# Keys and values of an attention computed ahead in units and kept in DRAM, with the chain of Q on ScalarE

## The chip, the core and the metric

One core of a Trainium2 chip runs the whole program. TensorE (PE) multiplies, the vector engine (DVE), ScalarE (ACT) and GpSimd (POOL) work on tiles in SBUF (DVE and ACT in PSUM too), and SyncE (SP) issues most DMAs. Each engine takes its instructions in order and waits on semaphores. The metric is the device time of one execution in microseconds (us), lower being better; the time before is the median of three runs.

## The reference, cut to what matters

Four batches of 512 rows of 512, each with a context of 512 rows of 256:

```python
x = x + ssm(ctx, layernorm(x))              # conv, 16 states scanned over 512 steps, 512 channels
x = x + ternary_ffn(layernorm(x))           # 512 -> 2048 -> 512, gelu, rows rounded to 8 bits
x = x + attention(layernorm(x), ctx)
x = x + moe(layernorm(x))                   # 8 experts, top 2, and a shared one

def attention(h, ctx):                      # 16 heads of 128; Wk, Wv: 256 x 2048, Wq: 512 x 2048
    q = rmsnorm((h @ Wq).reshape(B, 512, 16, 128), gq)
    k = rmsnorm((ctx @ Wk).reshape(B, 512, 16, 128), gk)
    v = (ctx @ Wv).reshape(B, 512, 16, 128)
    return softmax(q @ k.T * 128 ** -0.5) @ v @ Wo       # per head, heads joined before Wo
```

Keys and values depend on the context and the weights alone, not on `h`.

## The kernel before, in words

All is float32 but the ternary feed-forward and the experts. The order on each engine is written out by hand; engines meet by semaphores that count the uses of PSUM banks: a ring of two for each of `px`, `ps` (`py`) and `pp`, a `full` and a `drained` count for each bank.

The program has a prologue, four turns (one for each batch) and the mixture of experts. The prologue runs the scan of batch 0 in TC = 8 rounds on DVE (`times_b`, `scans`, `times_c`, for i = 0 and 1), and in each round makes a piece of the ternary weights: `w_sums` on ACT, `ternary` on DVE, `w_turned` on PE, `w_out` on ACT. PE sums the states in `y_sum`. ACT makes the next round's exponentials in `decay`.

A turn b first ends the scan of its batch (`scan_end`), then runs the feed-forward (`in_quant`, `ffn1`, `ffn2_turned`, `ffn2`), with the front of the next batch's scan (`scan_a`, `scan_conv`, `scan_b`, `scan_c`, softplus) between them. Then the attention in NG = 8 groups of GH = 2 heads. `xn_turned` and `xn_out` put the normalised rows, transposed, into `xnT`. In a group, PE makes the rows of Q (`rows`, 32 matmul records of 256 columns), K and V (16 each) in `pp`, transposes K and Q, makes `scores`, `values`, and the `denominators`; and it projects the output of the group before (`out_proj(g, k0, h)`, two tiles in `px`), which DVE adds to `xc` (`add_out`). Around that, DVE copies the rows of Q and K out (`rows_out`), scales Q by the inverse root of its mean square (`mean_square`, `q_scale`), copies Q transposed, adds up the exponentials (`key_sums`) and inverts the denominators (`recip`). ACT squares Q and K, copies V and K transposed, and makes the exponentials, in which the factor of K stands as the scale. POOL raises the mean squares to -0.5 (`row_rms`).

In the three turns that have a next batch, DVE also runs its scan in the same groups: `times_b` and four scans for each of two states, `times_c`, `add_y`. The last turn has none of that. The first group of a turn has its own order and also a norm (`gate_norm` or `moe_norm`).

The weights of the next group are loaded by SP when the rows that used the old ones are `full`; `next_bc` loads the rows of B and C for the next states once `times_c` has read the old ones. All turns but the last are one hardware loop on each engine, and so are groups 1 to 7.

Of the kernel before, what the change touches and what calls it, by code (L numbers as in the profile page):

```python
# [12 lines left out]
F32 = mybir.dt.float32  # L13
# [17 lines left out]
GH = 2  # L31
# [18 lines left out]
SEG_SIZE = {"A": 2, "XQ": 4, "F1": 4, "B": 2, "F2T": 4, "F2": 1, "C": 4, "AP": 4, "W": NT * H, "POST": 4, "TERN": 5 * TC}  # L50
# [24 lines left out]
PP_OFF = {"Q": 0, "K": 2, "V": 4, "KT": 6, "QT": 7, "D": 6 + 2 * GH}  # L75
PP_FIRST = {**PP_OFF, "K": 0, "V": 2, "Q": 3}
PP_STEP = {"KT": 2, "QT": 2}
PP_USES = 6 + 3 * GH
assert PP_USES % 2 == 0


def program(nc, t):
    ctx = ExitStack()
    with ctx:
# [8 lines left out]
        x3_dram = nc.dram_tensor("x3_dram", (B, L, DM), F32).ap()  # L93

# [7 lines left out]
        minus_magic = sb("minus_magic", [P, 1])  # L102
        conv_w = sb("conv_w", [P, EC, DC])
# [50 lines left out]
        qraw, kraw = qk_raw[:, 0], qk_raw[:, 1]  # L154
# [7 lines left out]
        ctx_ssm = dsum  # L162

# [111 lines left out]
        sq_done = sem("sq_done")  # L275
        ssv_done = sem("ssv_done")
# [73 lines left out]
        dram = t  # L350

# [27 lines left out]
        def _(sp):  # L379
# [16 lines left out]
            def bc_store(s, turn_):  # L396
                if not isinstance(s, int):
# [12 lines left out]
            def w_load(which, g):  # L410
                name, dst, s, chunk = {"k": ("Wk", wk, wk_in, CC), "q": ("Wq", wq, wq_in, NC), "v": ("Wv", wv, wv_in, CC)}[which]
                src = dram[name].rearrange("(c p) w -> p c w", p=P)
                sp.dma_start(dst[:], src[:, :, bass.ds(g * GW, GW)]).then_inc(s, 16)

# [22 lines left out]
            def pair(j, which):  # L437

                for odd in range(2):
                    r = j * 2 + odd  # L440
                    sp.wait_ge(stage_used[odd], j)
                    w_stage(r, odd, which)
                    for i in range(GH):
                        sp.wait_ge(hc_done[i], r)
                        bc_load(bc_first[odd][:, i], (bc_odd_in if odd else bc_in)[i], r * GH + i)
# [1312 lines left out]
```

## Time and profile before

| | us |
|---|---|
| median of 3 runs (2214.78 to 2217.63) | 2215.62 |
| the profiled execution, its own time | 2218.66 |
| its span, first to last instruction | 2216.7 |
| PE busy | 1985.3 (90%) |
| DVE busy | 1661.4 (75%) |
| ACT busy | 953.3 (43%) |
| POOL busy | 172.7 (8%) |
| DMA moved | 122.79 MB |
| mean granted TensorE clock | 0.939 |

The span is what lies inside the trace; the execution's own time has 2.0 us more around it. Busy shares are means over stages with different limits, so the rows further down are cut by stage. In the trace a float32 matmul of 512 columns is two records of 0.43 us start to start; their durations overlap. A helper issues most matmuls, so that their line is always L1334, and the tiles tell them apart.

### The profile page before, as it was taken

To read this page: it belongs to the slowest core of one execution; us is meant where nothing else is said; L and a number is where in the kernel's file an instruction comes from. 1 tells how busy PE (TensorE), PEld (TensorE's weight loads), DVE (VectorE), ACT (ScalarE), POOL (GpSimd) and SP (SyncE) were. 2 spreads that over 40 slices of the span, in tenths; PEclk is the share of its full clock that TensorE was granted. 3 is DMA by queue.
4 is the path that set the end of the run, shared out by engine and by line. 5 is a ranking of instruction groups with operands and counts; after the bars stand their busy time and mean duration, and the time that the engine had idled before them with its cause. 6 is when DMAs were issued, how large, how long until landed. Compare 5 with 4: busy or idle time off the path is not lost.

```text
span 2216.7 us, 25518 instructions
## 1 busy us (share of the span) xinstructions
PE 1985.3 (90%) x7548; PEld 1155.7 (52%) x7548; DVE 1661.4 (75%) x2271; ACT 953.3 (43%) x2208; POOL 172.7 (8%) x120
## 2 busy tenths in 40 slices
PE   6545798999989889999898999996899999899999
PEld 2222345656654556656445565662556666454554
DVE  2999567999995789999867999998553434356555
ACT  3544255455543555555346455552443434221221
POOL 0000001100010110100101010010011101000000
PEclk8777898999999999999998999998999999899999
DMA  3223011212111011222101121221122323100100
GB/s 121 76 76 114 10 40 33 72 57 80 62 57 58 32 54 51 77 62 76 67 20 38 54 79 57 76 66 38 48 58 53 75 51 67 48 32 6 39 19 19
DMA packets 90732, 122.79 MB, mean 55 GB/s; under 512 B 8880, under 2 KB 52528, under 8 KB 90176
## 3 DMA queue, kind: packets, MB, share of 16 engines
q1 hardware_dynamic: 79104, 113.89, 16.1%
q0 software_dynamic: 10768, 6.82, 2.2%
q10 hardware_dynamic: 816, 1.57, 0.2%
q8 instruction: 19, 0.31, 0.1%
q14 instruction: 25, 0.20, 0.0%
HBM read 119.90 MB, written 8.65 MB: 58 GB/s over the span
## 4 chain that ended last, share of the span: by engine, by line
issue 37%; PE 34%; DVE 24%; POOL 2%; DVEq 1%; DMA 1%; ACT 1%; POOLq 0%; SPq 0%; ACTq 0%
PE pp L1334 11%; PE px L1334 11%; DVE arena L959 10%; DVE arena L970 5%; PE ps L1334 5%; DVE arena L951 3%; PE pp L1555 2%; PE po L1334 2%; PE pd L1334 2%; DVE dsum L1192 1%; DVE qk_raw L1116 1%; DVE dsum L1188 1%; POOL bc L535 1%; POOL arena L541 1%; POOL rms L554 1%
## 5 line engine op out<-in xcount | busy, mean ns | idle before, releaser
L959 DVE TENSOR_TENSOR_SCAN arena<-arena 128x512 f32<-128x512 f32 x256 | 290.0, 1201 | 1.8
L1334 PE MATMUL px<-wo,oT 128*128 128x512 f32 x512 | 251.7, 616 | 23.6 <-DVE xc L1156 23.2
L1334 PE MATMUL ps<-qkT 128*128 128x512 f32 x512 | 252.9, 605 | 3.3 <-ACT hbuf L798 3.0
L798 ACT ACTIVATE hbuf<-ps,shift,rms 128x512 f32<-128x512 f32 x256 | 198.6, 777 | 127.4 <-PE ps L1334 119.9
L1334 PE MATMUL pp<-wq,xnT 128*128 128x256 f32 x1024 | 237.1, 391 | 2.9 <-issue 1.5
L786 ACT ACTIVATE dsum<-qk_raw 128x128 f32<-128x128 f32 x512 | 151.2, 296 | 185.4 <-DVE qk_raw L1116 185.4
L1156 DVE SCALAR_TENSOR_TENSOR xc<-px,rden,xc 128x512 f32<-128x512 f32 x256 | 187.6, 748 | 41.6 <-PE px L1334 33.7
L1334 PEld LDWEIGHTS pp<-wq,xnT 128*128 128x128 f32 x1024 | 198.0, 196 | 31.2 <-ACT xnT L773 4.1
L554 POOL TENSOR_TENSOR rms<-ssv,minus_half 128x8 f32<-128x8 f32 x64 | 105.0, 1640 | 960.1 <-DVE ssv L1170 960.1
L655 ACT ACTIVATE arena<-arena,a_neg 128x512 f32<-128x512 f32 x256 | 161.3, 709 | 21.5 <-DVE arena L959 16.6
L1334 PEld LDWEIGHTS ps<-qkT 128*128 128x128 f32 x512 | 90.9, 193 | 127.0 <-issue 76.8
L1334 PEld LDWEIGHTS px<-wo,oT 128*128 128x128 f32 x512 | 96.8, 197 | 105.5 <-issue 61.8
L1116 DVE COPY qk_raw<-pp 128x512 f32<-128x512 f32 x128 | 87.8, 686 | 69.9 <-PE pp L1334 69.7
L1334 PE MATMUL pp<-wk,ctx_att 128*128 128x256 f32 x512 | 121.0, 383 | 16.1 <-DVE qk_raw L1116 16.1
L1334 PE MATMUL po<-hbuf,v_sb 128*128 128x512 f32 x256 | 130.7, 592 | 0.0
L869 ACT ACTIVATE oT<-px 128x512 f32<-128x512 f32 x72 | 43.0, 597 | 201.5 <-PE px L1334 201.5
L951 DVE TENSOR_TENSOR arena<-arena,bc 128x2048 f32<-128x2048 f32 x56 | 127.7, 2280 | 2.3 <-DVE v_sb L921 2.0
L1334 PE MATMUL pd<-hbuf,v_sb 128*128 128x512 f32 x256 | 126.0, 615 | 0.0
L1334 PEld LDWEIGHTS pp<-wk,ctx_att 128*128 128x128 f32 x512 | 95.3, 190 | 49.4 <-issue 28.3
L1334 PE MATMUL pp<-wv,ctx_att 128*128 128x256 f32 x512 | 116.8, 380 | 2.6 <-DVE qk_raw L1116 2.5
L970 DVE TENSOR_TENSOR arena<-arena,bc 128x2048 f32<-128x2048 f32 x52 | 118.0, 2274 | 0.0
L977 DVE TENSOR_TENSOR arena<-arena 128x2048 f32<-128x2048 f32 x48 | 110.0, 2291 | 3.4
(198 smaller groups left out, 2972.4 us busy)
## 6 DMA issues: line engine op xcount, KB each, us to landing
bc<-bc_dram SPq DMA_DIRECT2D x56, 512.0 KB, 5.3
wq<-in_Wq SPq DMA_DIRECT2D x32, 512.0 KB, 4.7
wo<-in_Wo SPq DMA_DIRECT2D x32, 512.0 KB, 3.3
hbuf<-in_w SPq DMA_DIRECT2D x8, 1024.0 KB, 5.2
wk<-in_Wk SPq DMA_DIRECT2D x32, 256.0 KB, 2.5
wv<-in_Wv SPq DMA_DIRECT2D x32, 256.0 KB, 2.5
xs<-in_x SPq DMA_DIRECT2D x4, 1024.0 KB, 5.1
xnT<-bc_dram SPq DMA_DIRECT2D x8, 512.0 KB, 7.3
```

Of the source, the lines that this page charges most:

```text
L554: nc.gpsimd.tensor_tensor(rms[:, j], ssv[:, j], minus_half[:, 0:NT * GH], ALU.pow).then_inc(rms_done, 1)
L655: nc.scalar.activation(dA[i][:, e], delta[:, e], ACT.Exp, scale=a_neg[:, e, bass.ds(g * GH + i, 1)]).then_inc(exp_done[i], 1)
L786: nc.scalar.activation(squared[:, i], raw[:, k, h * D:(h + 1) * D], ACT.Square, accum_out=ss[:, j, i:i + 1]).then_inc(sq_done, 1)
L798: nc.scalar.activation(pT[:, h, k], ps[s_use % 2][:], ACT.Exp, bias=shift[:, 0:1], scale=rms[:, 1, k * GH + h:k * GH + h + 1]).then_inc(p_ ...
L951: V.tensor_tensor(hb[i], du, bc_i[:, 0:1, :].broadcast_to((P, EC, L)), ALU.mult).then_inc(dbu_done[i], 1)
L959: V.tensor_tensor_scan(hb[i][:, e], dA[i][:, e], hb[i][:, e], 0.0, ALU.mult, ALU.add).then_inc(scan_done[i], 1)
L970: V.tensor_tensor(dst, hb[i], bc_i[:, 1:2, :].broadcast_to((P, EC, L)), ALU.mult).then_inc(hc_done[i], 1)
L977: V.tensor_tensor(u, u, hb[i], ALU.add).then_inc(y_added, 1)
L1116: V.tensor_copy(dst[:, 2 * j:2 * j + 2, :].rearrange("p t w -> p (t w)"), pp[bank][:]).then_inc(pp_drained[bank], 1)
L1156: V.scalar_tensor_tensor(xc[:, k], px[bank][:], rden[:, h, k:k + 1], xc[:, k], ALU.mult, ALU.add).then_inc(px_drained[bank], 1)
L1334: return nc.tensor.matmul(out, lhsT, rhs, start=first, stop=last, **kw)
L1555: m = nc.tensor.transpose(pp[bank][:, k * P:(k + 1) * P], raw[:, k, h * D:(h + 1) * D], ident[:])
```

## The change

The keys and values of one batch and group are a unit U = 8b + g. A unit makes the rows of K, squares them, makes the rows of V, transposes K, and stores K (transposed, with its gain) and V in DRAM. Twelve units are made in the prologue (one and two per round in turn), four in the feed-forward of each of the first three turns, eight in that of the last. A group loads its two tiles. On ACT, a unit's rows of K are copied out and squared in their PSUM bank; DVE has no part in it. The inverse roots of a turn's units are one POOL instruction.

In a group the rows of Q stay in PSUM; ACT squares them there, makes the mean, scales them from PSUM to SBUF and copies Q transposed. The denominators go to `px`. DVE's order is new. The stages for the stores are `wo` and `wq` in the prologue and `xnT` in a turn. The turns are written out on SP and POOL, the prologue's rounds on all but DVE. PE's order in a turn and in a group, ACT's part of a unit, and SP's:

```diff
+            def kv(U, groups, loads):
+                pe.wait_ge(ctx_att_in, loads * 16)
+                pe.wait_ge(wk_in, U * 16 + 16)
+                for j in range(2):
+                    kv_rows(U, groups, "K", j, wk)
+                pe.wait_ge(wv_in, U * 16 + 16)
+                for j in range(2):
+                    kv_rows(U, groups, "V", j, wv)
+                pe.wait_ge(k_rows, U * 2 + 2)
+                for h in range(GH):
...
+                        m = nc.tensor.transpose(pp[bank][:, k * P:(k + 1) * P], kraw[:, k, h * D:(h + 1) * D], ident[:])
+            for r in range(TC):
+                for U in round_units(r):
+                    kv(U, 0, U // NG + 1)
+                for i in range(GH):
+                    y_sum(r, i)
+                w_turned(r // 2, r % 2, 1 if r < HG else 2)
...
                 if scan:
                     scan_a(b + 1, turn_, 0)
+                    scan_a(b + 1, turn_, 1)
                 scan_end(b, turn_)
                 if scan:
-                    scan_a(b + 1, turn_, 1)
                     scan_conv(b + 1, turn_, 0)
+                kvs(0, 1 if scan else 2)
                 in_quant()
                 ffn1(0)
...
                 ffn1(1)
                 if scan:
                     scan_b(b + 1, turn_)
+                else:
+                    kvs(2, 3)
...
                 ffn2_with_turned(1)
+                kvs(*((1, 2) if scan else (3, 5)))
                 ffn2_with_turned(2)
+                kvs(*((2, 3) if scan else (5, 7)))
                 ffn2(3, 0, 4)
+                kvs(*((3, 4) if scan else (7, 8)))
...
+                    if is_first(g):
+                        xn_turned()
+                        q_rows(0)
+                        q_rows(1)
+                    else:
+                        q_rows(0)
                         out_proj(g - 1, 0, 0)
+                        q_rows(1)
                         out_proj(g - 1, 0, 1)
                         out_proj(g - 1, 2, 0)
                         out_proj(g - 1, 2, 1)
+                    q_turned(0)
+                    q_turned(1)
                     scores(0, 0)
```

```diff
+            def kv_out(U, groups, stages):                  # ACT
+                for j in range(2):
...
+                    nc.scalar.activation(kraw[...], pp[bank][:], ACT.Copy).then_inc(k_rows, 1)
...
+                            m = nc.scalar.activation(slot, slot, ACT.Square, accum_out=ss_k[...])
...
+                nc.scalar.activation(ssv_k[...], ss_k[:], ACT.Identity, bias=eps[:, 0:1], scale=1.0 / D).then_inc(k_means, 1)
+                for j in range(2):
...
+                    nc.scalar.activation(stages[1][...], pp[bank][:], ACT.Copy).then_inc(pp_drained[bank], 1)
+                for h in range(GH):
...
+                    nc.scalar.activation(stages[0][:, h], pp[bank][:], ACT.Copy, scale=kgain[:, 0:1]).then_inc(pp_drained[bank], 1)
...
                 def xn_out():
+                    act.wait_ge(k_stored, units_after(b) * 16)
+                    act.wait_ge(v_stored, units_after(b) * 16)
...
+                        decays(0)                           # a later group
+                        squares(0)
+                        decays(1)
+                        squares(1)
+                        mean_squares()
+                    q_out()
+                    for h in range(GH):
+                        qT_out(h)
                     exps(0)
...
+                    if not (isinstance(g, int) and g == NG - 1):          # SP, in group(g)
+                        sp.wait_ge(ps_full[1], (G + 1) * (GH * NT // 2))
+                        kv_load(G + 1)
+                        sp.wait_ge(po_full, (G + 1) * GH)
+                        v_load(G + 1)
```

DVE in a later group is now `times_b(0)`, `add_out(0, 0)`, `times_b(1)`, `add_out(0, 1)`, `add_out(2, 0)`, `add_out(2, 1)`, `scans(0)`, `key_sums(0)`, `scans(1)`, `key_sums(1)`, `times_c(0)`, `recip(0)`, `recip(1)`, `add_y(0)`, `times_c(1)`, `add_y(1)`. In the first group `gate_norm` stands behind `recip(1)`. In the prologue ACT's round is `w_sums`, `kv_out`, `decay(0)`, a second `kv_out` in every other round, `decay(1)`, `w_out`.

## Rows read from the trace of the kernel before

**Rows 1.** Stretches: prologue, a feed-forward with scan, a group with scan, one without.

```profile
core 0: us, PE busy (x) PEld busy (x) DVE busy (x) ACT busy (x) POOL busy (x), PEclk, DMA share, GB/s
65.00:231.00 166.00, 90.72 (x367) 45.56 (x368) 161.32 (x147) 71.44 (x132) 0.79 (x1) 0.74 0.25 89
231.00:341.00 110.00, 94.71 (x383) 47.86 (x382) 68.75 (x105) 49.30 (x62) 9.31 (x4) 0.90 0.08 28
434.39:473.43 39.04, 38.47 (x146) 24.48 (x145) 37.65 (x46) 20.35 (x57) 3.28 (x3) 1.00 0.23 67
1677.52:1715.75 38.23, 38.22 (x145) 24.56 (x145) 16.38 (x32) 15.45 (x49) 5.50 (x5) 1.00 0.28 62
```

**Rows 2.** Instructions in order of time, PE, end of turn 0's feed-forward (start, duration).

```profile
325.63 3.62 PE L1334 MATMUL pp<-wk,ctx_att 128*128 128x256 f32 x16
...
340.75 9.34 PE L1334 MATMUL pp<-wq,xnT 128*128 128x256 f32 x32 [0.73 <-issue]
```

**Rows 3.** The same view, PE, a steady group with scan.

```profile
482.78 1.04 PE L1555 MATMUL pp<-ident,qk_raw 128*128 128x128 f32 x8
483.66 3.88 PE L1334 MATMUL ps<-qkT 128*128 128x512 f32 x8
...
499.38 7.15 PE L1334 MATMUL pp<-wq,xnT 128*128 128x256 f32 x32
```

**Rows 4.** The same view, ACT, a square and a copy out.

```profile
341.14 0.29 ACT L786 ACTIVATE dsum<-qk_raw 128x128 f32<-128x128 f32 x1
...
483.42 0.69 ACT L792 ACTIVATE qkT<-pp,kgain 128x512 f32<-128x512 f32 x1 [1.91 <-PE pp L1555]
```

**Rows 5.** The same view, PE, start and end of the prologue's rounds.

```profile
69.67 1.02 PE L1334 MATMUL pd<-arena,ident 128*128 128x512 f32 x2
...
233.74 1.88 PE L1334 MATMUL ps<-arena,ident 128*128 128x512 f32 x4
...
237.17 0.27 PE L1412 MATMUL px<-ident,w_scale 128*128 128x128 f32 x1
...
239.53 0.22 PE L1334 MATMUL px<-minus_bf,v_sb 128*128 128x128 bf16 x1
```

**Rows 6.** The same view, ACT, the end of round 1 and what follows.

```profile
107.66 0.60 ACT L682 ACTIVATE ws<-px 128x512 f32 x1 [10.08 <-PE px L1412]
...
110.97 0.63 ACT L670 ACTIVATE qk_raw<-hbuf 128x512 f32<-128x512 f32 x1
```

**Rows 7.** DMA issues: queue, times issued, KB each, median us to landing.

```profile
bc<-bc_dram SPq DMA_DIRECT2D x56, 512.0 KB, 5.3
...
x_dram<-xc SPq DMA_DIRECT2D x4, 1024.0 KB, 7.6
```

**Rows 8.** Instructions in order of time, DVE, group 1 and a steady group.

```profile
393.21 1.40 DVE L1156 SCALAR_TENSOR_TENSOR xc<-px,rden,xc 128x512 f32<-128x512 f32 x2
...
478.16 1.65 DVE L1178 TENSOR_SCALAR qk_raw<-qk_raw,rms 128x128 f32<-128x128 f32 x8
...
482.13 1.61 DVE L1156 SCALAR_TENSOR_TENSOR xc<-px,rden,xc 128x512 f32<-128x512 f32 x2 [0.17 <-PE px L1334]
...
504.69 2.29 DVE L977 TENSOR_TENSOR arena<-arena 128x2048 f32<-128x2048 f32 x1
506.90 0.68 DVE L1116 COPY qk_raw<-pp 128x512 f32<-128x512 f32 x1
```

**Rows 9.** The same view, PE, the last turn's feed-forward.

```profile
1535.87 3.92 PE L1447 MATMUL ps<-ident,hbuf 128*128 128x128 f32 x16 [10.80 <-DVE hbuf L1079]
...
1552.34 1.97 PE L1464 MATMUL ps<-ident,qkT 128*128 128x128 f32 x8 [5.00 <-DVE qkT L1099]
...
1586.63 3.62 PE L1334 MATMUL pp<-wk,ctx_att 128*128 128x256 f32 x16
...
1595.48 7.15 PE L1334 MATMUL pp<-wq,xnT 128*128 128x256 f32 x32 [0.73 <-ACT xnT L773]
```

**Rows 10.** Stretches around a wait of PE (columns as in the first group).

```profile
371.00:375.00 4.00, 1.22 (x9) 0.75 (x7) 3.83 (x7) 0.00 (x0) 0.00 (x0) 1.00 0.00 0
375.00:380.00 5.00, 5.00 (x16) 3.31 (x16) 4.27 (x13) 0.97 (x4) 0.46 (x1) 0.59 0.00 0
```

More of the change, by code:

```diff
@@ L563, in turn @@
                     log_error(b + 1)
-                else:
+                key_rms(units_before(b), units_after(b))
+                if not scan:
                     for i in range(2, 4):
@@ L708, in _ @@
             d_times_u(0)
-            def pair(j, which, last=False):
-                for odd in range(2):
-                    w_sums(j, odd, which)
-                    if not (last and odd):
-                        for i in range(GH):
-                            decay(0, j * 2 + odd + 1, i)
-                    w_out(j, odd, which)
-            with act.Fori(0, HG // 2) as j:
-                pair(j, 1)
-            for j in range(HG // 2, TC // 2):
-                pair(j, 2, last=j == TC // 2 - 1)
+            for r in range(TC):
+                j, odd, which = r // 2, r % 2, 1 if r < HG else 2
+                units = round_units(r)
+                w_sums(j, odd, which)
+                kv_out(units[0], 0, stages_first)
+                if r + 1 < TC:
+                    decay(0, r + 1, 0)
+                for U in units[1:]:
+                    kv_out(U, 0, stages_first)
+                if r + 1 < TC:
+                    decay(0, r + 1, 1)
+                w_out(j, odd, which)
             gate_silu(0, 0)
@@ L843, in group @@
                     exps(1)
+                    if is_first(g) and scan:
+                        d_times_u(b + 1)
                     for h in range(GH):
@@ L1214, in group @@
                             times_b(b + 1, g, 1)
+                        key_sums(G, 0)
+                        if scan:
                             scans(b + 1, g, 1)
-                        key_sums(G, 0)
-                        key_sums(G, 1)
-                        recip(0)
+                    else:
+                        if scan:
+                            times_b(b + 1, g, 0)
+                        add_out(g - 1, 0, 0)
+                        if scan:
+                            times_b(b + 1, g, 1)
+                        add_out(g - 1, 0, 1)
+                        add_out(g - 1, 2, 0)
+                        add_out(g - 1, 2, 1)
+                        if scan:
+                            scans(b + 1, g, 0)
+                        key_sums(G, 0)
+                        if scan:
+                            scans(b + 1, g, 1)
+                    key_sums(G, 1)
+                    if scan:
+                        times_c(b + 1, g, 0)
+                    recip(0)
+                    recip(1)
+                    if is_first(g):
                         if scan:
```

454 lines of the change are left out of this document (244 added, 210 removed).

## Prediction

> **What bounds the kernel now.** I read the stages first. In the prologue the vector engine (DVE) is busy 161 of 166 us and TensorE (PE) 91; in the scan batches' feed-forward stage PE is busy 95 of 110; in a steady attention group with a scan beside it PE is busy 38.5 and DVE 37.7 of 39.04; in the last batch, without a scan, PE is busy all 38.23 [rows 1]. So PE sets the pace of attention, nearly everywhere of the feed-forward, and not of the prologue. Then the instructions in order of time, for what follows what. The chain of waits gives PE 34%, DVE 24% and "issue" 37% of the span, too coarse here.
>
> **The change conserves PE work.** All 32 units of keys and values are still computed: 7.8 us of PE each: K rows 3.62 with their tail of 0.16, so 3.46 [rows 2], V the same, four transposes twice, 0.44 each [rows 3]. It leaves 32 groups and goes to 12 places in the prologue, 3 x 4 in the scan batches' feed-forward, 8 in the last one's. The sum is what each group gives back minus what each place costs.
>
> **A unit's price.** With ScalarE (ACT) free, from the unit's start: K0 to 1.7, K1 to 3.5; ACT takes K0 after 0.17, copies (0.6 to 0.7) and squares four times (0.29 each) [rows 4], so V0 starts only at 4.0, ends 5.7; K1's bank is free at 6.0, V1 ends 7.7; KT0 8.2; KT1 waits for V1's copy and takes 8.6 to 9.1. PE is held 9.1 us for 7.8 of work, ACT 9.9. Squares that read and write PSUM have no row; 0.29 is the SBUF one, bounds 0.2 to 0.4, that is 8.3 to 10 per unit.
>
> **Prologue, 12 units.** PE waits there for `times_c` each round. A round costs it two `y_sum` (3.43 each) [rows 5] and `w_turned`: 2.4 in the last four rounds [rows 5]; in the first four ACT drains it from 107.66 to 110.97 [rows 6], with the transposes ahead 3.7. The first unit stands behind ACT's `w_sums` (four of 0.62) [rows 6] and holds PE 10.2; a second one, behind a `decay`, ends at 20.5. So rounds of one unit take 10.2 + 6.9 + 3.7 = 20.8, of two 31.1; later 19.1 and 29.4 (`w_sums` is shorter). PE becomes the bound: DVE needs about 21 a round. Round 0 starts at 70.7, where the first sums end [rows 5], and takes 9.1 + 6.9 + 3.7 = 19.7; then 31.1 + 20.8 + 31.1 + 19.1 + 29.4 + 19.1 + 29.4 = 180.0, end at 270.4 against 239.7 [rows 5]: **+30.7**. Bounds: with units perfectly packed 12 x 7.8 + 8 x 9.95 = 173, end 243.5, +4; with ACT's two chains serial and some half clock, +45. Filling PE's idle also takes away the half clock after each, which is counted by using full-clock rows. SP's next weights are asked for one phase ahead; the inverse roots of 12 units are one POOL instruction of 96 columns. Now two of 8 columns take 3.28 [rows 1], which makes 1.64 flat to 19.7 by columns, starting some 12 before the end, so even with the diagonals behind it done before the convolution 20 later. Hidden.
>
> **Feed-forward with scan, 4 units.** Unit 0 stands before `in_quant`, where PE has just come from the convolution without a wait; units 1 and 2 between matmuls that followed each other. Nothing covers them: 3 x 9.1 = 27.3 (moving `scan_a` ahead of `scan_end` shifts work only). Unit 3 replaces K rows, V rows and a wait for the norm, from 325.63 to the Q rows at 340.75, 15.1 [rows 2]. New, from the same point: ACT is still in exp and ln, 3.8 more; K0 is taken there, so KT1 leaves PE at 10.9 and ACT at 11.9; `xn_out` now waits until the stores have landed, since `xnT` is their stage: no 512 KB store has a row, 1 MB takes 7.6 [rows 7], so 3.8 to 7.6, I take 4.7; then 2.6 for the copies: 19.2. +4.1. Queued behind that wait on ACT are the squares of Q and the `decay` that DVE's scans want; both are counted below from the Q rows on. `xs` is loaded behind SP's same wait and is wanted 30 later. Sum **+31.4** a batch.
>
> **A group with scan.** DVE loses 4 row copies, 8 scalings, 2 copies of Q, the mean squares: 2.7 + 1.6 + 1.4 + 0.3 = 6.0 (0.68 a copy, 1.65 the scalings) [rows 8]. PE loses 7.8. But PE's filler is gone. From the start of the Q rows, t = 0: `recip(1)` of the group before ends near 0.5; DVE does `add_y`, `times_c`, `add_y`, `times_b`, 2.2 each [rows 8], to 9.45 with their self-waits; `add_out(0,0)` to 10.8; `times_b` to 13.0; its next result frees px0 at 13.8. PE: Q rows and the first `out_proj` to 8.6; then it needs px0, free at 10.2: `out_proj(0,1)` to 12.0; idle to 13.8; then tile by tile with DVE (0.86, hand-over 0.17, 0.75) [rows 8]: `out_proj(2,1)` ends 17.4; transpose and ACT's copy of Q to 18.8; scores, values and denominators 15.7 as before, 483.66 to 499.38 [rows 3]. The loop closes at 34.5, with DVE waiting a microsecond for the last denominator. 39.03 - 34.5 = 4.5 saved. ACT's chain is inside it: squares of Q1 at 8.8 to 10.2, mean 10.4, POOL 1.64 and hand-overs to 12.2, eight scalings 14.4 (0.2 to 0.3 each; no row from PSUM), before 17.4. If it were later by over 3 it would be paid. Seven groups: **-31.5** a batch.
>
> Each unit also stores and loads 1 MB, 64 MB more over the kernel beside 123; in a group the DMA engines are busy 0.23 [rows 1], so the bandwidth is there and only order counts. SP's new waits: V's load waits for the last value product, and `next_bc(0)` is queued behind it, so that row of B and C is asked for at -0.5 instead of -3. It lands after 5.3 alone [rows 7], up to about 7.5 behind V; wanted at 7.2. bc 1, asked for at 5.0, is wanted at 10.8. Taken as just in time.
>
> **First group.** From the start of its Q rows (half clock, as now): scores at 16.9; 15.7 of PE work, plus 1.0 for the `decay` that stands between the two heads' exps, to 33.6; `recip` 0.5, the norm 4.4, three passes and `times_b` at 2.2, `add_out` 1.3: 48.6. Now that `add_out` ends at 394.6, 53.8 after 340.75 [rows 2, 8]. In a steady group it ends at 10.8 in place of 12.3, so 1.5 of the 5.2 is counted there already: **-3.7**, bounds 0 (a chain as long as now) and -7.8 (all PE work given back).
>
> **Last batch.** Units 0 and 1 go into the 10.8 wait [rows 9]: 18.3 plus a cold start, +8.5. Unit 2 into the 5.0 wait [rows 9], but behind a gelu: +4.9. Units 3 to 6: 4 x 9.15 = 36.6. Unit 7 in place of 1586.63 to 1595.48 [rows 9]: 9.9 + 4.4 + 2.3 = 16.6 against 8.9, +7.8. Sum +57.8. Group there: PE Q rows and `out_proj` to 14.1, both transposes and copy of Q to 15.5 (q chain 14.4), then 15.7: 31.2 against 38.23, x 7 = -49.2; first group -1.0. **+7.6**.
>
> **Sum.** 30.7 + 3 x (31.4 - 3.7 - 31.5) + 7.6 = 30.7 - 11.4 + 7.6 = +26.9. The profiled execution took 2218.66 (span 2216.7 and 2.0 around it), so 2245.6; it lay 3.0 over the median of the runs, 2215.62, so **2242**.
>
> **TensorE's clock.** In 371 to 375 PE was busy 1.22; in the 5 us behind it the granted clock was 0.59, 1.2 GHz for most of it [rows 10], against 1.00, 2.4 GHz, through groups with at most 0.57 idle [rows 1]. The new group has idles of 1.7 and 1.8 within five, in between. I take no fall: both are shorter than the one in the rows. The Trainium skill (TensorE: Matmul & The Clock Gate, "A second HAM failure mode: psum-queue depth-cycling") tells of a kernel whose short idles between groups of matmuls, from cycling through PSUM banks, made the clock swing between both levels; that speaks for the third rival.
>
> The Trainium skill (DMA: Bandwidth & Descriptors, "Anatomy of one DMA") gives a fixed 2.0 us plus bytes by 436 GB/s and says most of the fixed part is the write's receipt, longest for HBM; by it a 512 KB store would take 3.2 in place of my 4.7 and each of the four batches would be 1.5 shorter, 6 in all. The 7.6 measured for 1 MB [rows 7] is above the 4.4 that it gives there, so for stores the trace doesn't agree.
>
> **Rivals.**
> 1. The forecast, 2229 to 2257 with its unit bounds: 0.47.
> 2. Faster: the group is bound by DVE's own 31.7 plus 0.3, not by the hand-overs, since DVE runs ahead of PE in them. 21 x 2.5 = 52 less: 2190. For it: now DVE idles only 1.4 of 39. Against: `add_out` still waits for PE and PE for it. It decides the sign when the group is under 33.2 (26.9 / 21 less). 0.17.
> 3. Slower still: the clock falls in each scan group, 5 us at 0.59 lose 2.05 [rows 10]: 21 x 2.05 = 43, 2285. For it, the two idles in a row; against, neither is as long as the one that showed it. 0.16.
> 4. No change: the prologue packs its units (+4 in place of +30.7): 2215. For it: ACT is busy only 71 of 166 there [rows 1]. Against: two banks and an in-order ACT. 0.08.
> 5. bc or V lands late by 1 to 2 us a group: 2263 to 2284. 0.12.
>
> Range 2195 to 2288, leaving out most of rival 2 and the far ends of 3 and 5. This kernel's runs tell a change from 0.2%, 4.4 us. Faster: rival 2 and the lower half of 4, 0.20; same 0.05; slower 0.75.
>
> **What would show it.** Steady groups with scan 34.5 apart (Q rows to Q rows), 31.2 in the last batch; PE waiting for `add_out` on px twice per group; the last `w_turned` near 270 and almost no PE wait for `times_c`; from the first DVE norm of a scan batch to its first Q rows 31 more than now; `xn_out` waiting for DMA. Wrong if units overlap so that PE is held under 8.3 each, or the group is off 34.5 by more than a microsecond: that term is multiplied by 21.

## The result and the profile after

The change made the kernel slower: 2270.03 us (median, 2264.91 to 2272.74) against 2216.62, ratio 1.0238 (95% interval 1.0217 to 1.0259), +53 where the prediction had +27. The sign was right and the time lies in the range; the size of the change was half of what came. The profiled execution of the changed kernel has a span of 2271.1.

Stretches of the kernel after, the same four kinds as in [rows 1] (start:end, length, then the busy time of PE, PEld, DVE, ACT, POOL, the granted clock, DMA share, GB/s):

```profile
core 0: us, PE busy (x) PEld busy (x) DVE busy (x) ACT busy (x) POOL busy (x), PEclk, DMA share, GB/s
65.00:271.00 206.00, 183.05 (x892) 126.19 (x892) 164.44 (x149) 147.68 (x414) 12.26 (x1) 0.97 0.49 160
271.00:407.00 136.00, 115.01 (x472) 67.41 (x472) 68.13 (x103) 70.84 (x147) 18.81 (x6) 0.90 0.22 74
484.70:519.66 34.96, 31.49 (x107) 17.34 (x106) 32.18 (x30) 18.60 (x47) 1.64 (x1) 1.00 0.29 90
1760.53:1792.11 31.58, 31.21 (x107) 17.35 (x106) 10.51 (x16) 13.60 (x39) 3.87 (x4) 1.00 0.39 91
```

TensorE (PE) now fills the prologue, 183 of 206 where it was 91 of 166. In a steady scan group it is no longer the only bound: PE 31.5 and the vector engine (DVE) 32.2 of 34.96, and each waits for the other.

To see where the 53 sit I mark each turn by GpSimd's first power of its norm, and divide it at the Q rows (`L1334` before, `L1444` with `wq` after). A "Q rows" mark is the start of that group's first Q matmul. All times in us, from the traces:

| | before, turns 0, 1, 2 | after, turns 0, 1, 2 |
|---|---|---|
| norm to first Q rows | 80.17, 78.93, 78.78 | 112.77, 111.13, 111.98 |
| Q rows 0 to 1 | 38.82, 36.60, 38.60 | 37.38, 37.64, 36.14 |
| Q rows 1 to 2 | 41.74, 41.85, 42.16 | 39.97, 40.10, 39.71 |
| a steady group | 39.03 | 34.96 |
| Q rows 7 to next norm | 70.93, 71.36, 63.12 | 66.29, 67.74, 57.92 |

The first mark moved from 260.58 to 294.58 (+34.0), the turns by +4.4, +7.8 and +2.7, the last turn with the experts by +5.5: 54.4, the difference of the spans. The prediction had 30.7, three times -3.8, and 7.6. So the miss of 26 lies in the three scan turns, +14.9 in place of -11.4, and most of it where no unit stands, in the attention groups.

PE at the end of turn 0's feed-forward, for [rows 2] (start, duration, form, count, idle before and its releaser):

```profile
371.16 3.62 PE L1444 MATMUL pp<-wk,ctx_att 128*128 128x256 f32 x16
374.98 3.72 PE L1444 MATMUL pp<-wv,ctx_att 128*128 128x256 f32 x16 [0.20 <-ACT pp L809]
...
379.88 3.62 PE L1444 MATMUL px<-w2t,qk_raw 128*128 128x512 bf16 x16
383.33 3.62 PE L1444 MATMUL pp<-wk,ctx_att 128*128 128x256 f32 x16
389.09 5.41 PE L1444 MATMUL pp<-wv,ctx_att 128*128 128x256 f32 x16 [2.14 <-ACT pp L809]
...
395.68 1.04 PE L1666 MATMUL ps<-ident,hbuf 128*128 128x128 f32 x8
404.34 1.97 PE L1666 MATMUL ps<-ident,hbuf 128*128 128x128 f32 x8 [7.63 <-ACT xnT L929]
407.35 9.97 PE L1444 MATMUL pp<-wq,xnT 128*128 128x256 f32 x32 [1.04 <-ACT xnT L929]
424.29 1.97 PE L1701 MATMUL pp<-ident,qk_raw 128*128 128x128 f32 x8 [6.98 <-ACT qk_raw L951]
```

Unit 2 holds PE from 371.16 to 379.88, 8.72. Unit 3 holds it 12.35: V's rows wait 2.14 behind softplus' exp and ln on ScalarE (ACT), and then run partly at the lower clock (5.41 for 3.6; the granted clock was 0.72 in 389 to 395). Next PE waits 7.63, and at the next step 6.98; the Q rows between take 9.97 for 32 matmuls that take 7.15 in [rows 9]. What ACT waited for, and when SP had issued it:

```profile
403.69 1.09 ACT L929 ACTIVATE xnT<-ps 128x512 f32<-128x512 f32 x2 [7.13 <-DMA kt_dram<-xnT]
```

```profile
394.53 0.39 SPq L457 DMA_DIRECT2D wv<-in_Wv  x1
394.96 0.47 SPq L460 DMA_DIRECT2D ctx_att<-in_ctxT  x1
395.53 0.41 SPq L477 DMA_DIRECT2D v_dram<-xnT  x1
396.64 0.36 SPq L481 DMA_DIRECT2D kt_dram<-xnT  x1
```

DVE in the same first group, for the chain behind [rows 8]: it stands idle 15.98 before its first scan, until ACT has done squares, mean, a table load and a decay.

```profile
402.62 2.29 DVE L1112 TENSOR_TENSOR arena<-arena,bc 128x2048 f32<-128x2048 f32 x1 [0.24 <-DVE arena L1100]
420.90 4.57 DVE L1120 TENSOR_TENSOR_SCAN arena<-arena 128x512 f32<-128x512 f32 x4 [15.98 <-ACT arena L755]
```

PE in a steady group, for [rows 3]:

```profile
484.70 3.70 PE L1444 MATMUL pp<-wq,xnT 128*128 128x256 f32 x16
488.24 1.88 PE L1444 MATMUL px<-wo,oT 128*128 128x512 f32 x4
489.95 3.62 PE L1444 MATMUL pp<-wq,xnT 128*128 128x256 f32 x16
495.13 1.98 PE L1444 MATMUL px<-wo,oT 128*128 128x512 f32 x4 [1.56 <-DVE xc L1309]
498.65 3.96 PE L1444 MATMUL px<-wo,oT 128*128 128x512 f32 x8 [1.53 <-DVE xc L1309]
502.44 1.04 PE L1701 MATMUL pp<-ident,qk_raw 128*128 128x128 f32 x8
503.73 4.09 PE L1444 MATMUL ps<-qkT 128*128 128x512 f32 x8 [0.25 <-ACT qkT L961]
```

The two waits on px are there, as forecast, and the clock stays at 1.00.

### The profile page after: what moved, and what is told of

It reads as the page before. It is cut to its first block, busy times and chain, and to the rows that moved or that the text cites. A ratio compares the mean times of both kernels' runs of the same rounds, so it can differ in the third digit from the quotient of the medians.

```text
span 2271.1 us, 25731 instructions
## 1 busy us (share of the span) xinstructions
PE 2006.8 (88%) x7548; PEld 1143.2 (50%) x7548; DVE 1480.7 (65%) x1759; ACT 1094.3 (48%) x2656; POOL 167.1 (7%) x94
## 4 chain that ended last, share of the span: by engine, by line
PE 61%; issue 16%; DVE 11%; ACT 9%; DMA 2%; DVEq 1%; POOL 0%; ACTq 0%; SPq 0%; POOLq 0%
PE px L1444 17%; PE ps L1444 16%; PE pp L1444 12%; PE po L1444 6%; PE pd L1444 6%; DVE arena L1112 3%; DVE arena L1138 2%; DVE arena L1131 2%; DVE xc L1309 2%; ACT pp L809 2%; PE ps L1598 1%; ACT hbuf L967 1%; DMA kt_dram<-xnT 1%; PE pp L1563 1%; ACT dsum L801 1%
## 5 line engine op out<-in xcount | busy, mean ns | idle before, releaser
L1444 PE MATMUL px<-wo,oT 128*128 128x512 f32 x512 | 262.3, 639 | 97.7 <-DVE xc L1309 97.2
L1444 PE MATMUL ps<-qkT 128*128 128x512 f32 x512 | 259.9, 620 | 13.3 <-ACT qkT L961 7.0
L967 ACT ACTIVATE hbuf<-ps,shift,rms_k 128x512 f32<-128x512 f32 x256 | 198.8, 778 | 138.4 <-PE ps L1444 131.2
L1444 PE MATMUL pp<-wq,xnT 128*128 128x256 f32 x1024 | 244.3, 394 | 3.8 <-ACT xnT L929 3.8
L1444 PEld LDWEIGHTS pp<-wq,xnT 128*128 128x128 f32 x1024 | 199.7, 198 | 45.1 <-issue 17.7
L1444 PEld LDWEIGHTS px<-wo,oT 128*128 128x128 f32 x512 | 90.5, 197 | 236.4 <-DVE xc L1309 204.7
L1444 PEld LDWEIGHTS ps<-qkT 128*128 128x128 f32 x512 | 91.9, 194 | 146.9 <-ACT hbuf L967 74.6
L1444 PE MATMUL pp<-wv,ctx_att 128*128 128x256 f32 x512 | 123.6, 396 | 22.9 <-ACT pp L809 22.9
L1444 PE MATMUL po<-hbuf,v_sb 128*128 128x512 f32 x256 | 130.7, 592 | 0.0
L939 ACT ACTIVATE qk_raw<-pp 128x128 f32<-128x128 f32 x256 | 67.4, 278 | 130.4 <-PE pp L1444 130.4
L1444 PE MATMUL pp<-wk,ctx_att 128*128 128x256 f32 x512 | 118.6, 385 | 5.0 <-DMA ctx_att<-in_ctxT 4.9
L1444 PE MATMUL pd<-hbuf,v_sb 128*128 128x512 f32 x256 | 123.0, 603 | 0.0
L1444 PEld LDWEIGHTS pp<-wv,ctx_att 128*128 128x128 f32 x512 | 96.9, 196 | 49.6 <-issue 22.1
L647 POOL TENSOR_TENSOR rms<-ssv,minus_half 128x8 f32<-128x8 f32 x32 | 56.8, 1776 | 865.0 <-ACT ssv L944 865.0
L1248 DVE SCALAR_TENSOR_TENSOR hbuf<-px,fsc,ws 128x512 f32<-128x512 f32 x64 | 47.9, 750 | 93.4 <-PE px L1444 90.3
```

Of the source, the lines that this page charges most:

```text
L647: nc.gpsimd.tensor_tensor(rms[:], ssv[:], minus_half[:, 0:NT * GH], ALU.pow).then_inc(rms_done, 1)
L939: nc.scalar.activation(qraw[:, k, h * D:(h + 1) * D], pp[bank][:, i * GW + h * D:i * GW + (h + 1) * D], ACT.Square, accum_out=ss[:, h * NT ...
L967: nc.scalar.activation(pT[:, h, k], ps[s_use % 2][:], ACT.Exp, bias=shift[:, 0:1], scale=rms_k[:, bass.ds(G * (GH * NT) + (h * NT + k), 1) ...
L1248: V.scalar_tensor_tensor(hbuf[:, k % 2, j * 512:(j + 1) * 512], bank, fsc[:, 0, 4, k:k + 1], ws1[:, j * 512:(j + 1) * 512], ALU.mult, ALU. ...
L1444: return nc.tensor.matmul(out, lhsT, rhs, start=first, stop=last, **kw)
```

## The experiments

"Over before" is always the median less the median of the kernel before in the same comparison; the changed kernel has +53.4. Three of the four questions are about the scan turns: the store, the first group, the order in a steady group; the fourth is what the kernel before could win by the same means.

**1. The first decays ahead of the squares (e1).**

```diff
                     if is_first(g):
                         xn_out()
+                        decays(0)
                         squares(0)
                         squares(1)
                         mean_squares()
-                        decays(0)
```

> Changed kernel, but in the first group of a scan turn ScalarE runs the four decays of state 0 before the squares of Q instead of after the mean of squares. In the changed kernel ScalarE stands idle for 6.96 us there (waiting for the Q rows), and the decays with their table load are 3.8 us long. Theory A (the first group is a chain of latencies through ScalarE: squares, mean, table load, decays, scaled Q): scaled Q starts 1.6 us earlier, because only the power on GpSimd (1.64) then stands between mean and scaling; VectorE's 16 us of idle time before the scans becomes idle time elsewhere, since its next work (key sums, then the second state's scans) waits for ScalarE's exps and second decays. Gain 1.6 a turn, about 5 in all: 2265. Rival B (the 16 us in which VectorE waits for the first decay are themselves what the group costs, VectorE being the bound behind it): first add_out 5 us earlier in each of three turns, 15 in all: 2255.

2255.80, ratio 1.0176 (1.0149 to 1.0204), +37.9 over before. The total would suit B, but the trace doesn't put all of it there. Q rows 0 to 1 took 32.91, 33.67 and 34.84, which is 9.7 less in the three turns; Q rows 1 to 2 took 39.45, 39.61 and 39.71, almost unmoved.

```profile
401.13 8.68 PE L1444 MATMUL pp<-wq,xnT 128*128 128x256 f32 x32 [1.19 <-ACT xnT L929]
414.78 1.97 PE L1701 MATMUL pp<-ident,qk_raw 128*128 128x128 f32 x8 [4.97 <-ACT qk_raw L951]
416.58 4.70 PE L1444 MATMUL ps<-qkT 128*128 128x512 f32 x8
```

```profile
448.18 1.40 DVE L1309 SCALAR_TENSOR_TENSOR xc<-px,rden,xc 128x512 f32<-128x512 f32 x2
```

The wait for the scaled Q fell from 6.98 to 4.97 in every turn, A's latency. In turn 0 the scores behind it went from 5.88 to 4.70, and the Q rows ahead of it, which the edit doesn't touch, from 9.97 to 8.68; the granted clock of 401 to 421 was 0.84 and 0.83, against 0.70 and 0.64 in 407 to 427 of the changed kernel. So the first `add_out` ended 48.4, 49.2 and 50.4 after the Q rows in the three turns, in place of 52.9, 53.2 and 51.7. Some 7.5 of the span's gain lie ahead of the Q rows, where the edit does nothing: in 332.8 to 352.8 the clock was 1.00, and 0.84 and 0.82 in 334.6 to 354.6 of the changed kernel's own trace. Neither theory: 2.0 a turn of latency, and in turn 0 another 2.5 of clock, of which 1.3 are the Q rows', ahead of what the edit moves.

**2. Both decays ahead, both scans ahead of the key sums (e1b).** As above with `decays(1)` too (taken from between `exps(0)` and `exps(1)`), and on DVE `scans(b + 1, g, 1)` ahead of `key_sums(G, 0)`.

> Changed kernel, but in the first group of a scan turn both states' decays (table load 1.28, then 2.56 and 2.54) stand before the squares of Q, inside ScalarE's idle 6.96 us, and VectorE runs both scans before the key sums. Theory A: now nothing of the scan stands between scores and exps, so key sums end 3 to 4 us earlier, and times_c, the norm and the add_out behind them with it; distance from the Q rows of group 0 to the end of the first add_out 52.85 falls to about 48, and Q rows 0 to 2 take 72 to 73 instead of 77.4. Gain 5 a turn (3 to 8), 15 in all: 2255. Rival B (group 0 is held by the half clock of its matmuls and by waits for the softmax, not by the scan's place): gain under 2 a turn, 2265 or more.

2260.87, ratio 1.0195 (1.0178 to 1.0212), +42.9. Q rows 0 to 1: 33.49, 33.43, 34.60; 1 to 2: 40.47, 39.71, 40.45. Rows 0 to 2 took 73.96 in turn 0 and the first `add_out` ended at 49.0, both nearly A's numbers; the total lies between the two theories. But e1 has that `add_out` at 48.4 already, so what this run moves beyond e1 brought it no earlier:

```profile
442.98 2.47 DVE L1140 BATCH_NORM_STATS2 ln_st<-xs 128x6 f32<-128x512 f32 x4
...
456.58 1.39 DVE L1308 SCALAR_TENSOR_TENSOR xc<-px,rden,xc 128x512 f32<-128x512 f32 x2
457.37 8.48 PE L1442 MATMUL px<-wo,oT 128*128 128x512 f32 x12 [6.06 <-DVE xc L1308]
```

The norm of the next batch's input stands in front of `add_out`; PE waits 6.06 and then runs 12 matmuls in 8.48. That is what Q rows 1 to 2 are long from.

**3. Another order of DVE in a group (e3).** Nothing is added or left out.

```diff
+                        add_out(g - 1, 0, 1)
                         if scan:
                             times_b(b + 1, g, 0)
-                        add_out(g - 1, 0, 0)
+                        add_out(g - 1, 2, 0)
                         if scan:
                             times_b(b + 1, g, 1)
-                        add_out(g - 1, 0, 1)
-                        add_out(g - 1, 2, 0)
                         add_out(g - 1, 2, 1)
...
                     if scan:
                         add_y(b + 1, g, 0)
                         times_c(b + 1, g, 1)
+                    add_out(g, 0, 0)
+                    if scan:
                         add_y(b + 1, g, 1)
                 for_groups(dve, group)
-                add_out(NG - 1, 0, 0)
```

> Changed kernel, but VectorE adds the output projection in another order: the first pair of a group before the last add_y of that group, the second pair before the first times_b, the third between the two times_b, the fourth after both. Same instructions, same number. Theory A (a steady group of 34.96 is a loop of hand-overs: VectorE is busy 33.1 us of it, TensorE stands 1.56 and 1.53 us at the output projection waiting for banks that VectorE drains late): TensorE's two waits go, VectorE becomes the bound, a steady group takes 33.2 to 33.8; with the clock unchanged 1.2 to 1.7 less for 18 to 21 groups, 22 to 35 in all: 2240. Rival B (the loop is closed by ScalarE's Q chain behind the second Q rows, so TensorE waits for the scaled Q instead of for the banks): 34.5 to 35, total 2262 or more.

2227.96, ratio 1.0054 (1.0037 to 1.0070), +10.0: the largest single gain, 43. A steady group takes 33.32, and Q rows 1 to 2 fall from 40 to 36.4, since the first `add_out` no longer waits for the whole list. Theory A; the total is below A's 2240 by the second groups (10) and by the stretches ahead of the Q rows, where the edit does nothing (7.5 in the three turns, as in e1). (The 33.1 of the expectation was a sum of durations, in which neighbours overlap; the stretches have 32.18 in the changed kernel.)

```profile
507.21:540.54 33.33, 31.23 (x106) 17.43 (x106) 31.80 (x31) 18.59 (x47) 1.64 (x1) 1.00 0.29 94
```

DVE is busy 31.80 of it. Of PE's two waits one is gone, the other is 1.73.

**4. The last unit's loads behind its stores (e4).** In `kv_dma`, where `ctx_next` is given, `w_load("v", ...)` and `ctx_load(...)` are issued after the store of `kt_dram[U]`.

> Changed kernel, but for the last unit of a turn the loads of the next Wv and of the next context are issued behind the two stores instead of ahead of them. The store of KT that ScalarE waits for before it may write the transposed input (7.13 us) was issued 396.64 and had landed 403.7, with 512 KB of V and some 0.75 MB of loads ahead of it in the same queues. Theory A (the store is late because of what stands ahead of it): it lands 2 us earlier, and Q rows of group 0 start 2 us earlier, 2 a turn, 6 in all: 2264. Rival B (a store's landing is a fixed time from its issue, 6 to 7 us in whatever company): 0, 2270.

```profile
402.76 1.09 ACT L932 ACTIVATE xnT<-ps 128x512 f32<-128x512 f32 x2 [3.22 <-DMA kt_dram<-xnT]
```

The wait for the store was 7.13, 6.74 and 6.36 in the three turns and is 3.22, 3.21 and 3.21: theory A. 2261.07, ratio 1.0197 (1.0180 to 1.0214), +43.1, 10 less, where A had 6; 10.6 by the waits. The same edit moves the load of batch 1's context in the prologue behind two stores: PE waits 6.67 for it there and not 4.93, and the first mark is 3.0 later. The store of 512 KB takes 3.15 from its issue with one like it ahead, and 7.05 with loads of 768 KB ahead of both. The Trainium skill (DMA: Bandwidth & Descriptors, "Anatomy of one DMA") fits DMAs on GpSimd's path by 2.0 us plus the bytes at 436 GB/s; the estimate by it is 3.2. These stores are SP's, for which the section gives no fit, but at 512 KB the trace agrees with it; the prediction had found that it didn't for a store of 1 MB.

**5. The last unit ahead of the last FFN product (e5), and with it the subtraction on DVE (e6).**

```diff
-                kvs(*((2, 3) if scan else (5, 7)))
+                kvs(*((2, 4) if scan else (5, 7)))
                 ffn2(3, 0, 4)
-                kvs(*((3, 4) if scan else (7, 8)))
+                kvs(*((4, 4) if scan else (7, 8)))
```

ACT's `kv_outs` likewise, ahead of `softplus_exp`. For e6 also, in DVE's `softplus_end`, with GpSimd's `log_error` gone from the turn:

```diff
                 dve.wait_ge(sp_act, 3 * s + 3)
+                if not (isinstance(s, int) and s == 0):
+                    dve.wait_ge(sp_step, 4 * s + 1)
+                    V.tensor_tensor(hb[0], hb[1], dA[0], ALU.subtract).then_inc(sp_pool, 1)
                 dve.wait_ge(sp_pool, s + 1)
```

> Changed kernel, but the last unit of a scan turn runs right behind the third one, ahead of the last FFN product (TensorE and ScalarE in the same order), so that softplus' exp and ln no longer stand before its copies. Theory A (the 12.35 us that unit 3 holds TensorE, instead of 8.72, and the wait of 7.13 for its store are what the unit costs too much): unit 3 takes 8.7, its stores land long before the transposed input is written, so 3.6 and part of the 7.1 come back; Q rows of group 0 start some 6 us earlier in each scan turn, 18 in all: 2252. Theory B (the FFN's end and the norm behind it become the chain: ffn_out, statistics, power on GpSimd, then a small VectorE instruction of 4.46 us that runs beside GpSimd's subtraction of 4.51 us, all of them 8.7 us later than now): normalized input ready at 403.2 to 405, Q rows at 407, where they stand now: 0, 2270.

> As e5_unit3_early, and the subtraction of 128x2048 in softplus is done by VectorE (2.29 us, behind the norm) instead of by GpSimd (4.51 us, beside the norm). In the trace of both kernels the 128x4 VectorE instruction that runs beside it takes 4.46 us, against 0.16 otherwise. Theory (that collision sets the norm's end once unit 3 is out of its way): normalized input 4.3 us earlier than in e5, Q rows of group 0 at 402.8 against 407.35 now, 4.5 a scan turn, 13 in all: 2257. Rival (what VectorE gains it gives back, since the subtraction is now its own work ahead of the first times_b): no difference between e5 and e6.

e5: 2269.47, ratio 1.0219 (1.0202 to 1.0236), +50.3. e6: 2255.33, ratio 1.0163 (1.0147 to 1.0180), +36.2. Theory B for e5; e6 is 14 less than e5, as its theory had it (13). In e5, GpSimd and DVE side by side:

```profile
399.90 4.50 POOL L634 TENSOR_TENSOR arena<-arena 128x2048 f32<-128x2048 f32 x1
```

```profile
399.96 4.45 DVE L1153 SCALAR_TENSOR_TENSOR ln_nm<-ln_mv,ln_r 128x4 f32<-128x4 f32 x1 [1.12 <-POOL ln_r L643]
404.44 1.92 DVE L1164 TENSOR_SCALAR hbuf<-xc,ln_r,ln_nm 128x512 f32<-128x512 f32 x4
```

and in e6:

```profile
392.82 0.19 DVE L1154 SCALAR_TENSOR_TENSOR ln_nm<-ln_mv,ln_r 128x4 f32<-128x4 f32 x1 [1.12 <-POOL ln_r L643]
393.05 1.92 DVE L1165 TENSOR_SCALAR hbuf<-xc,ln_r,ln_nm 128x512 f32<-128x512 f32 x4
```

```profile
383.60 3.62 PE L1445 MATMUL px<-w2t,qk_raw 128*128 128x512 bf16 x16
393.65 3.60 PE L1667 MATMUL ps<-ident,hbuf 128*128 128x128 f32 x16 [6.43 <-DVE hbuf L1165]
```

An instruction over four columns takes 4.45 beside GpSimd's, and 0.19 without it. From norm to Q rows e5 needs 113.51, 113.35, 112.14 (so the 8.7 of unit 3 and the store's wait come back as a later norm), e6 105.96, 109.12, 107.86.

**6. e3's order with the norm moved too (e7), and with e4 and the subtraction (e8).** On DVE `gate_norm(b + 1, 3 * b + 3)` goes from behind `recip(1)` to behind `scans(b + 1, g, 1)`, ahead of `key_sums(G, 0)`; the decays stand as in e1b. GpSimd's order:

```diff
                 def group(g):
                     G = b * NG + g
+                    if is_first(g) and scan:
+                        rstd(0, 3 * b + 3)
                     row_rms(G)
-                    if is_first(g):
-                        rstd(0 if scan else 3, 3 * b + 3)
+                    if is_first(g) and not scan:
+                        rstd(3, 3 * b + 3)
```

> e3_dve_order with the decays of e1b_decays, and the norm of the next batch's input (statistics 2.47, aggregates, the power's round trip, 4.4 in all) moved from behind the reciprocals to ahead of the first key sums, where VectorE stands idle 7.49 us in e1b; GpSimd raises its power ahead of that of the Q rows. In e1b TensorE waits 6.06 us for the first add_out of group 0, and runs at half clock behind it (12 matmuls in 8.48), and Q rows 1 to 2 take 40.5. Theory A (that wait is the norm's 4.4 and the long order in front of add_out): the wait is below 1.5, the clock stays, Q rows 1 to 2 take 33.5 to 34.5 as in a steady group, 0 to 1 take 33.4: 5 a turn below e3, 15 in all: 2213. Rival B (the first group is held by the round of the first scores and softmax, VectorE catches up anyway): as e3 with e1b's 3 a turn: 2221.

> e7_order_norm with the loads of the last unit behind its stores (e4) and the subtraction on VectorE. Theory: the parts add up, since they lie in different stretches of the turn: e4's stores landed 3.14 us after issue against 5.4 to 7.1, 3.5 a turn, and the subtraction changes nothing while the norm is ready before unit 3 ends (normalized input from 393.6, unit 3 until 395.7): 10 below e7, 2203, which is under the kernel before. Rival (an earlier store only moves the wait to the transposes or the Q rows' own loads): as e7, 2213.

e7: 2229.33, ratio 1.0055 (1.0036 to 1.0074), +10.2, no better than e3, where the theories had 2213 and 2221. e8: 2224.89, ratio 1.0025 (1.0016 to 1.0035), +5.7; from norm to Q rows it takes 10.0 less than e7 in the three turns, as its theory had it, but its first mark is 2.4 later, by the context's load as in e4. Q rows 1 to 2 became 33.32, a steady group; Q rows 0 to 1 became 39.15, 38.99 and 39.99. My order on GpSimd did it (e7):

```profile
420.06 1.01 POOL L643 TENSOR_TENSOR ln_r<-ln_ve,minus_half 128x4 f32<-128x4 f32 x1 [23.18 <-DVE ln_ve L1150]
421.04 1.64 POOL L647 TENSOR_TENSOR rms<-ssv,minus_half 128x8 f32<-128x8 f32 x1
```

The power for Q stood behind one whose input DVE finished at 419.98, and PE waited 11.44.

**7. GpSimd's order put back (e9); the early unit in place of the late loads (e10).** e9 is e8 without the diff above; e10 is e9 without e4's edit and with e5's.

> e8_order_norm_loads, but GpSimd raises the power of the Q rows ahead of that of the norm again (the norm's place on VectorE stays). In e7 and e8 Q rows 0 to 1 took 38.7 to 40.0 instead of 33.4, TensorE waiting 11.44 for the scaled Q: GpSimd stood in the norm's power until VectorE's statistics, behind both scans, were done at 419.8, and the Q rows' power, ready to start at 414.5, came behind it at 421.1. Theory (that order alone ate what e7 won behind it): Q rows 0 to 1 fall to 33.5 and 1 to 2 stay at 33.3, 5.3 a scan turn, 16 in all: 2209. Rival (the norm's statistics or the scans hold VectorE at the first key sums whatever GpSimd does): 38 stays, 2225.

> As e9_combined, but in place of the loads behind the stores the last unit stands ahead of the last FFN product (e5, e6). The stretch from a turn's first norm to its Q rows was 106.0 to 109.1 in e6 and 107.5 to 108.9 in e8, so both ways lead to about the same place. Theory: within 6 us of e9. Rival (the stores' wait in e9 costs clock in the first group, which e10 has not, its idle time being shorter, 3.77): 3 a turn less than e9, 2200.

e9: 2209.83, ratio 0.9955 (0.9938 to 0.9972), 10.7 under before. e10: 2207.53, ratio 0.9942 (0.9925 to 0.9959), 13.0 under. Q rows 0 to 1 are 33.50, 33.51, 33.53 in e9, as expected, with this on GpSimd:

```profile
415.35 1.94 POOL L650 TENSOR_TENSOR rms<-ssv,minus_half 128x8 f32<-128x8 f32 x1 [15.02 <-ACT ssv L945]
421.15 1.01 POOL L646 TENSOR_TENSOR ln_r<-ln_ve,minus_half 128x4 f32<-128x4 f32 x1 [3.86 <-DVE ln_ve L1152]
```

e9 hit its number, 2209. e10 is within 6 of e9; its rival is not borne out, Q rows 0 to 1 being 34.90 to 35.03.

**8. The kernel before with the subtraction on DVE (e11).** The edit of e6 in the other kernel. The rows of the kernel before that it starts from:

```profile
330.43 4.51 POOL L541 TENSOR_TENSOR arena<-arena 128x2048 f32<-128x2048 f32 x1
```

```profile
330.50 4.46 DVE L992 SCALAR_TENSOR_TENSOR ln_nm<-ln_mv,ln_r 128x4 f32<-128x4 f32 x1 [0.47 <-POOL ln_r L550]
...
336.19 3.83 PE L1520 MATMUL ps<-ident,hbuf 128*128 128x128 f32 x16 [4.12 <-DVE hbuf L1003]
```

> The kernel before, with softplus' subtraction on VectorE instead of GpSimd, as in e6. In its trace TensorE waits 4.12 us for the normalized input, behind the 4.46 us that the small VectorE instruction takes beside GpSimd's 4.51 [rows 8]. Theory (the collision sets the Q rows' start in both kernels, and a part of what e9 wins is open to the kernel before too): Q rows of group 0 start some 3.5 us earlier, less 2.29 of VectorE's time ahead of its first times_b; 1 to 4 a turn, 3 to 11 in all: 2211. Rival (VectorE, busy without a gap behind it in this kernel, gives all of it back): 2217 to 2221.

2205.95, ratio 0.9934 (0.9918 to 0.9951), 14.6 under before, above the 3 to 11 of the theory; the two profiled executions differ by 8.1 only. From norm to Q rows: 74.63, 73.33, 72.94, some 5.6 less in each turn; PE waits 0.24 for the norm, and the Q rows take 7.14 in place of 9.34 [rows 2]. Between the Q rows 7 and the next norm 3.4 and 2.9 came back in two of the turns. In turn 0, 1.0 of it is the last output projection, with the granted clock at 0.56 against 0.68 in its 10 us, and 2.4 is DVE, which starts the last two additions to `xs` after 4.83 idle in place of 2.45, with nothing in the profile that it waited for. Why either differed stays open. So one edit in the kernel before reaches what the changed kernel reaches with five.

**9. The gate product after the last add_out (e12).** In e10, `gate_y(b + 1)` behind the last `add_out` of a turn instead of ahead of three of them.

> e10_combined_unit3, but at the end of a scan turn VectorE adds the last three pairs of the output projection before it multiplies y by the gate. In e10 an add_y of 2.29 takes 4.67 at the first turn's end while GpSimd builds the diagonals (3.61), in the changed kernel four gate products of 0.68 take 4.58 beside it (5.74), and the add_out, which read a bank of PSUM, keep their 0.75 beside it; TensorE waits 3.86 and 4.65 there. Theory (TensorE's wait for the banks is on the path at the turn's end, the gate product is not yet): 1 to 2 us from the last Q rows of a turn to the next norm, in three turns, 3 to 6 in all: 2203. Rival (scan_a waits for the gate product, so what the banks win the gate loses): 2207, as e10.

2214.92, ratio 0.9984 (0.9974 to 0.9993), 4.4 under before, so 8.6 worse than e10. The rival, and more:

```profile
685.22 2.49 DVE L1182 TENSOR_TENSOR arena<-arena 128x512 f32<-128x512 f32 x4
...
687.83 10.07 PE L1441 MATMUL ps<-dsum,ipT 128*128 128x512 f32 x16 [3.33 <-DVE arena L1182]
```

`scan_a` waits 3.33 for the gate product, and its 16 matmuls then take 10.07 in place of the 7.03 that they take in e10. The waits ahead of it, 3.86 and 2.22, are not longer than e10's 3.86 and 4.65, so what the banks won went to this wait and to the clock behind it.

## Why the prediction was right in sign and half the size

**The prologue: the sum came out, in part by luck.** Twelve units, +31.1 at the last `w_turned` (270.8 against 239.7), forecast +30.7. But seven of the eight rounds were shorter than forecast, 6.3 in all (30.0 for 31.1, 19.9 for 20.8, 27.8 for 29.4), the first began 1.8 late, and round 5 took 34.6 for 29.4: the load of the next batch's context, which the sum didn't have, came too late for its second unit.

```profile
204.33 5.64 PE L1444 MATMUL pp<-wk,ctx_att 128*128 128x256 f32 x16 [4.93 <-DMA ctx_att<-in_ctxT]
```

The mark behind it is 3 later still, because all of `scan_a` now stands ahead of `scan_end`; "moving `scan_a` shifts work only" is true of the turn, and shows as a later norm and a shorter stretch behind it.

**Right: a unit holds PE longer than it works.** 8.72 against a forecast of 9.1 (bounds 8.3 to 10). The squares from PSUM to PSUM took 0.26 to 0.27, not 0.29. In the last turn those that follow each other take 8.8 to 9.0.

**Near by luck: the last turn,** +5.5 for +7.6, by two errors that cancel: the feed-forward grew by 49.4 in place of 57.8, and the rest shrank by 43.9 in place of 50.2 (a group 31.58, forecast 31.2).

**Failed: "First group, -3.7".** This term was mis-sized: once the seven steady groups are taken out, at the 4.07 that each gave back, the stretch from the Q rows to the next norm came out at +0.3, +4.1 and -2.0 in the three turns, 13.5 worse in all (a part of turn 1's because the kernel before had its Q rows 0 to 1 at 36.60 there, and the forecast took turn 0's for all). The step said that the chain to the first `add_out` would be 48.6; it was 52.9. Its lines on DVE:

```profile
445.17 0.18 DVE L1332 RECIPROCAL rden<-den 128x4 f32<-128x4 f32 x1 [2.16 <-ACT den L978]
...
458.88 1.40 DVE L1309 SCALAR_TENSOR_TENSOR xc<-px,rden,xc 128x512 f32<-128x512 f32 x2
```

Two things in that chain were mis-priced. Scores came 18.75 after the Q rows and not 16.9, because ACT does the decays with their table load between mean and scaling. And from the scores to the end of the last reciprocal it took 19.3 and not 17.2, since PE, having waited 7.63 and then 6.98, ran the first eight score matmuls in 5.88 for 3.88 (granted clock 0.64 in 417 to 427). The slow Q rows were priced (9.34, "half clock, as now"; they took 9.97), and so were the norm, the three passes, `times_b` and `add_out` behind the reciprocal, 14.9 for 14.5. e1 bears this out: with the decays ahead of the squares the chain ends at 50.4 in turn 2, whose Q rows take 9.96, and at 48.4 in turn 0, where they take 8.68. The decays' place is 2.0 of it and the clock the rest; why the clock differs from turn to turn stays open. e3 and e9 then move what had been priced but need not stand ahead of `add_out`: Q rows 0 to 2 go from 77.4 to 66.8.

**Slightly off: unit 3, "+4.1".** It was 8.9 to the Q rows: the unit 12.35 in place of 10.9, and a store taken at 4.7 from the issue that landed after 6.3 to 7.1. I had priced the store by its size, and the queue ahead of it was the price (e4). In the stretch from norm to Q rows only 1.3 of it shows (+32.7 on average for +31.4), since the later mark gives some back: 3.8 in the three turns.

**Slightly off, times 21: "a steady group 34.5".** 34.96. Scores start 19.03 after the Q rows (forecast 18.8), and 15.93 later come the next (15.7). The shape was right to the two waits, 1.56 and 1.53 for a forecast 1.6 and 1.8. So each of the 21 gave back 4.07 and not 4.5: 9.0.

13.5 + 3.8 + 9.0 = 26.3, what was missed in the scan turns.

**The rivals.** The forecast's own band, 2229 to 2257, was left by 13. Rival 2 (the group bound by DVE at 32) did not hold in this kernel, but e3 shows that it was mostly a matter of order: 33.32 with DVE busy 31.80, still 1.5 above DVE's own work. With that I ought to have said from which order it decides. Rival 3: the clock is 1.00 in the steady groups; it did fall, in the first group of each turn and in the feed-forward, where no rival had it. Rival 4 is out by the prologue. Rival 5: bc lands after 5.1, and the only wait of DVE for it in the trace is one of 0.16.

**What the change is worth.** With five mends the changed kernel is 13 under before (e10); but the kernel before with one of them is 14.6 under (e11), and no run tried whether its first group has more to give. A steady group gives back 4.1, with e3's order 5.7, for a unit that costs 8.7 in the feed-forward, or 2.6 in the prologue (31.1 by 12). That is the balance the prediction drew, and no run here turned it.

## What to carry to other kernels

Work moved out of a balanced loop saves only what the second busiest engine allows (here 4.1 of 7.8), and costs its full length wherever its engine has no idle to take it (8.7 in the feed-forward, 2.6 in the prologue); price both before the details. When the loop is close between two engines, write down the order of the lesser one too: the same instructions took 34.96 or 33.32. And price the first turn of a loop by itself, store, queue and clock included: half of this miss was there, and behind its two 7 us waits the matmuls took 2 to 3 us more (9.97 for 7.15, 5.88 for 3.88). A long wait doesn't always cost that: in e5 PE waits 10.69 and the Q rows behind it take 7.17, with a granted clock of 0.50 in 398.5 to 408.7 and 1.00 in 408.7 to 417.2.

## What the runs showed of the hardware

A DVE instruction of four columns, with two inputs in SBUF, took 4.45 us when GpSimd had just begun a 128x2048 subtraction of 4.50, and 0.19 in the run without it. Beside GpSimd's 5.74 for the diagonals the first of four gate products took 2.78 and the others 0.68, while `add_out`, one of whose inputs is a bank of PSUM, kept its 0.75. The Trainium skill (SBUF — State Buffer, "SBUF: two separate sides") tells of an exclusive lock on a pair of ports, taken for a whole instruction by GpSimd or, when the GpSimd instruction reads SBUF, by a DVE operation with two SBUF inputs; these traces agree with it. It was in the trace of before, in one instruction of each scan turn whose duration stood out 27 times over its median, and the prediction did not look for it.
